# A gathering graph kernel: GpSimd starts each group of four gathers only after the group before has landed

## The reference

```
deg_out = segment_sum(edge_weight, src); deg_in = segment_sum(edge_weight, dst)
norm = edge_weight * rsqrt(deg_out[src] * deg_in[dst] + EPS)
# a layer, done twice (W6, then W7):
xt  = x @ W
msg = xt[src] * norm[:, None]
agg = segment_sum(msg, dst, num_segments=n_nodes)
h   = relu(agg + b)
```

## Time and profile before

| | us |
|---|---|
| median of three runs | 3715.28 (3714.16 to 3717.88) |
| the profiled execution, whole | 3720.0 |
| its span in the trace | 3718.2 |
| POOL busy in the span | 2172.4 (58%) |
| PE busy in the span | 3030.2 (81%) |
| granted TensorE clock, mean | 0.90 of full |

### The profile page before, as it was taken

One profiled execution on the slowest core, in us unless ns is written; L12 is line 12 of the kernel. 1 busy time (PEld: TensorE's weight loads), 2 busy tenths in 40 slices (PEclk: granted clock), 3 DMA queues, 4 the chain that ended last, 5 costly groups with the idle time before them and its releaser, 6 DMA issues.

```text
span 3718.2 us, 52328 instructions
## 1 busy us (share of the span) xinstructions
PE 3030.2 (81%) x16152; PEld 2012.8 (54%) x16152; DVE 1803.2 (48%) x4528; ACT 1150.8 (31%) x4063; POOL 2172.4 (58%) x2090
## 2 busy tenths in 40 slices
PE   4777837888888888888885689888888888888998
PEld 3445514555555555555553356556555555555666
DVE  9989835666666666656542133223212324132334
ACT  5787834444444443444330011001000101002211
POOL 4666656666666666666664666666666666630000
PEclk8899967999898998999987789989998998988999
DMA  4331134544544545445456534654655454533221
GB/s 118 99 104 54 56 77 132 159 154 138 172 139 152 161 136 170 139 140 171 129 180 186 131 123 135 204 175 145 197 189 188 152 190 151 191 104 105 78 77 47
DMA packets 219543, 515.58 MB, mean 139 GB/s; under 512 B 62465, under 2 KB 129831, under 8 KB 208169
## 3 DMA queue, kind: packets, MB, share of 16 engines
q0 software_dynamic: 88704, 243.35, 22.8%
q1 hardware_dynamic: 124053, 262.34, 20.8%
q10 hardware_dynamic: 6500, 6.40, 0.6%
HBM read 384.88 MB, written 127.07 MB: 138 GB/s over the span
## 4 chain that ended last, share of the span: by engine, by line
PE 46%; issue 8%; another core or an unknown queue 6%; DVE 3%; DMA 2%; ACT 1%; POOL 1%; DVEq 1%; ACTq 0%; SPq 0%; POOLq 0%
PE ps L702 19%; PE ps L680 7%; PE ps L663 5%; PE ps L873 5%; PE ps L886 4%; PE ps L821 1%; PE ps L824 1%; POOL ringb L1960 1%; PE ps L642 1%; PE ps L809 1%; ACT ab L1737 1%; DMA t<-mbuf 0%; DVE ab L1303 0%; DMA x2d<-accb 0%
## 5 line engine op out<-in xcount | busy, mean ns | idle before, releaser
L1960 POOL DMA_INDIRECT ringb<-t,src x1848 | 1862.5, 1008 | 979.1 <-issue 496.5
L702 PE MATMUL ps<-xb,ab 125*128 125x256 f32 (+1 forms) x4700 | 1253.7, 407 | 83.3 <-issue 80.6
L702 PEld LDWEIGHTS ps<-xb,ab 125*128 125x128 f32 x4700 | 934.9, 203 | 358.5 <-issue 197.7
L680 PE MATMUL ps<-mlb 128*125 128x300 f32 x1260 | 484.1, 475 | 170.4 <-issue 67.9
L1737 ACT ACTIVATE ab<-ps 125x250 f32 x724 | 295.2, 408 | 797.3 <-PE ps L680 408.8
L663 PE MATMUL ps<-ringb,Sb 128*32 128x257 f32 (+1 forms) x3696 | 378.2, 417 | 141.9 <-issue 78.2
L680 PEld LDWEIGHTS ps<-mlb 128*125 128x125 f32 x1260 | 228.1, 205 | 335.7 <-issue 298.1
L1933 POOL TENSOR_TENSOR ab<-ab,wn 128x100 f32<-128x100 f32 x201 | 274.6, 1371 | 167.7 <-DVE ab L1086 167.7
L604 PE MATMUL ps<-ab 128*50 128x125 f32 x3228 | 222.7, 286 | 132.3 <-ACT ab L1659 45.0
L1270 DVE TENSOR_TENSOR mlb<-iof,rel 128x900 f32<-128x900 f32 (+1 forms) x231 | 232.2, 1005 | 172.5 <-remote 104.6
L1659 ACT ACTIVATE ab<-ab,wn 128x50 f32<-128x50 f32 x1212 | 288.8, 330 | 18.6 <-DVE ab L1086 18.6
(11 more groups left out here) (245 smaller groups left out, 2704.3 us busy)
## 6 DMA issues: line engine op xcount, KB each, us to landing
ad<-ab SPq DMA_DIRECT2D x42, 1600.0 KB
ab<-ad SPq DMA_DIRECT2D x42, 1600.0 KB
ringb<-t,src POOLq DMA_INDIRECT x1848
kvd<-mlb SPq DMA_DIRECT2D x50, 256.0 KB, 2.1
kvb<-kvd SPq DMA_DIRECT2D x50, 256.0 KB
x2t<-mlb SPq DMA_DIRECT2D x13, 500.0 KB
xb<-x2t SPq DMA_DIRECT2D x13, 500.0 KB, 8.2
xb<-in_x SPq DMA_DIRECT2D x10, 625.0 KB
```

What stands on the lines that cost most here:

```text
L680: e.matmul(PS[bank_of(t)][0:R, 0:HR], low[:, slot_of(t), :], high[:, slot_of(t), :], start=True, stop=True).then_inc(s_bld, 1)
L702: ins = e.matmul(PS[dense_bank(L, d)][:, 0:wd], lhs, X[0:R, k, 0:wd], start=k == 0, stop=k == NT - 1)
L1960: e.indirect_dma_start(msg[:, slot * QT + k, 0:width], None, table, bass.IndirectOffsetOnAxis(src[:, t:t + 1], 0)).then_inc(s_g[slot], 16)
```

## The change

One condition is added in front of each quad but the first of each pass: GpSimd waits until all four gathers of the preceding quad have landed, 64 counts of the preceding slot's semaphore. The count is exact for the quad: it takes in the 41 quads that each slot held in pass 0.

```diff
--- before.py
+++ after.py
@@ -1955,6 +1955,9 @@
                         e.wait_ge(s_mm, NQ)
                     elif j == 4:
                         e.wait_ge(s_flag, 1)
+                    if j >= 1:
+                        landed = (j - 1) % RQ
+                        e.wait_ge(s_g[landed], 64 * (L * len(range(landed, NQ, RQ)) + (j - 1) // RQ + 1))
                     for k in range(QT):
                         t = column(L, j) + k
                         e.indirect_dma_start(msg[:, slot * QT + k, 0:width], None, table,
```

## The result

| | before | after |
|---|---|---|
| median | 3716.58 us (3714.16 to 3720.15) | 4827.75 us (4820.07 to 4844.52) |
| ratio | | 1.2997, 95% interval 1.2974 to 1.3019 |
| profiled execution, whole | 3720.0 us | 4833.86 us |
| its span | 3718.2 us | 4832.1 us |

The change costs 1111 us. The forecast was +765 and its range ended at 4670: the direction and the mechanism were right, the size was not.

A forecast was written before the change was run, and what follows sets the result against it. PE was taken to set the pace, GpSimd following closely. Quiet cycles 1752 + 1484 plus load 313 gave 3549 us against 2779, +770 on 3720.0: 4490, rounded to 4480 us; range 4270 to 4670 us.

The forecast's parts named there:

- between and behind the passes: Stretches before, between and after the two passes: claimed to stay as they were, their work not being touched.
- What bounds it, and the direction: Both passes: PE sets the pace, GpSimd follows closely; added waits make GpSimd's line longer, so slower by over 0.2%, 96%.
- The quiet landing: At each quad's start without SP's load: the last gather lands 1.86 us after its descriptors are written.
- The load: Landings beside SP's large transfers: 92 quads caught, each 3.4 us later, 313 us in all.
- The descriptors: GpSimd's descriptor writing with gaps: thins a little in a longer pass, to 5.02 and 4.77 us a quad.
- GpSimd's own start after a wait: From the landing to the next quad's first gather: taken as 0.24 us, bounded by 0 and 0.98 us.
- the forecast's own spread: Whole kernel: load 130 to 450 us and start 0.1 to 0.4 us, about 4250 to 4660 us, chance 78%.
- (a): Rival at the quads' starts: the wait is mostly hidden, time within 0.2% of 3715 us; chance 2%.
- (b): Rival: fewer gathers in flight let PE's large products get `A` sooner, faster at 3632 us; chance 2%.
- (c): Rival: little load on the landing, 313 us shrinking to some 60, start in 0.1 us, 4170 us; chance 10%.
- (d): Rival: a store holds the whole quad, 7 us a caught quad, start 0.4 us, 4730 us; chance 8%.
- The sign that I named wrongly: In the profile after, almost none of the waits on GpSimd's gather line would be released by PE.

The follow-up runs named there:

- e1: Changed kernel with the wait for PE's slot moved to the last gather of the quad before, so no gather has two waits: 4542.64 us.
- e2: Changed kernel with the two waits in the other order, landing written before slot: 4545.17 us.
- e5: The changed kernel timed again, unaltered, on a chip where the kernel before takes 3684.11 us: 4818.39 us.
- e9: The changed kernel timed again, unaltered, on a chip where the kernel before takes 3366.01 us: 4836.35 us.
- e10: The kernel of e1 run again, on the chip of e9 beside the changed kernel: 4540.32 us.
- e11: Changed kernel with SP's stores and loads of A cut to a sixteenth, which leaves work out: 4659.45 us against 4836.35.
- e8: Changed kernel with GpSimd also held to four quads ahead of PE in place of six: 4814.72 us beside 4818.39.
- e7: Changed kernel with the landing wait at every second quad only: 4169.68 us, +486 beside the kernel before at 3684.11.
- e3: Kernel before with a second, always satisfied wait at each quad from the seventh on: 3365.61 us beside 3366.35, ratio 0.9997.
- e4: Changed kernel with the landing wait moved from a quad's first gather to its second: 3960.19 us, 594 us over the kernel before.
- e6: Changed kernel, but each quad waits for the landing of the quad before the last one: 3727.01 us beside 3684.11, ratio 1.0123.

## Why the prediction was wrong in size

By its own steps, in the profiled executions. The measured parts of a gap are means over all quads, worked out from the trace's landing events (the last landing of a quad less the end of its fourth gather, and the next start less that landing).

| term | forecast | measured |
|---|---|---|
| descriptors and their gaps, pass 0 and 1, a quad | 5.02, 4.77 us | 5.18, 4.76 us: +37 us |
| landing in the quiet | 1.86 us | 1.8 to 1.9 us |
| landing under load, in all | 313 us | about 360 us: +48 |
| from the landing to the next gather | 0.24 us | 0.86, 0.87 us: +286 |
| between and behind the passes | 0 | -22 |

The terms add up to 349 us. The profiled execution grew by 1114 us where the sum said 770, so 344 were missing; the forecast also counted 462 waits where there are 460, which is most of the difference.

- **What bounds it, and the direction: right.** A quad's serial line is longer than the step of 6.09 and 5.93 us, GpSimd has no cover for it, and PE becomes the one that waits, 653 us at line 663 alone. "Slower", forecast with 96%, came true, and the stretches outside the passes stayed but for 22 us.
- **The quiet landing: right.** 1.86 us from the earlier trace rows came back, with a median of 1.82 to 1.88 us in each pass of the result, e1, e2, e5, e9 and e10.
- **The load: nearly right.** 313 against some 360 us. 97 of the 460 landings are more than 1 us late, by 3.4 us in the mean, where the forecast had 92 with 3.4. The 200 GB/s and the single price of 3.4 us were rough, and e11 shows that only half of it comes from the largest transfers, so part of the agreement is luck.
- **The descriptors: a small error.** They were to thin out in a longer pass. In pass 0 the mean gather went from 1.043 us to 1.067, with DVE busy 877 of 2117 us. DVE's share alone, which the forecast took as the reason, doesn't explain this.
- **The failed step is GpSimd's own start after a wait.** The prediction bounded it by 0 and 0.98 us and took 0.24, "a little under the 0.30 us between two gathers, as the added wait also is an instruction of its own". The form was seen, and its price was taken from gathers without one. 0.24 is nearly right where the gather carries the landing wait (e1, e2, the first quads): 0.26 us as a rule, 0.92 at every ninth quad, 0.33 in the mean. With the wait in an instruction of its own it is 0.76 us, and 1.71 at every ninth quad, 0.86 in the mean. 0.62 us x 460 = 286 us of the 344 us that were missing. The separate instruction is 0.53 us of this, 245 us in all; the other 42 us stay in e1 and e2. e10 takes the instruction away and gets back 296 us on the chip of e9 (e1 and e2, on another chip than the result, 285 and 283), of which some 50 are descriptors: their mean in pass 0 also falls, from 5.18 to 4.96 us a quad. Why it falls is open.
- **The range failed for the same reason.** The known bound of 0.98 us was cut to 0.4 for the forecast's own spread. 0.98 on 460 quads is 340 us more than 0.24, which alone would have taken the forecast of 4480 to 4820. The spread that was stated was also added up too low: load 450 and start 0.4 together give 4480 + 137 + 74 = 4691, not 4660. A bound far from the value taken has to stay in the range when the term is multiplied by every quad.
- **The rivals.** (a) and (b) needed a landing within 1 us and fell with it. (c), little load, fell: landings under load cost 360 us. (d) came closest in time, 4730 us, but not by its mechanism: a late landing is late by 3.4 us in the mean, and by 7.2 at the most. PE's pace as a part of it is excluded by e5 and e9, and by e8 for the ring.
- **The sign that I named wrongly.** I expected almost no wait released by PE. The profile shows 136; by e1 they are landings with the wrong name.

What stays open: why every ninth start takes longer. It takes 0.95 us more in the changed kernel (and in e7, at the 25 of these quads that wait) and 0.66 us more in e1, e2 and e10, so it belongs to a start behind a landing and not to the separate instruction alone. e3, where nothing is waited for, has no such start. Nothing in these runs names its cause.

No version that does all the work is faster than the kernel before.

## What to carry to other kernels

Price a wait in a tight issue loop as the whole exposed line, the landing, plus the start after it, times every round, and see what lies beside the landing: one more gather in flight (e4) took away 60% of the loss and one more quad (e6) nearly all, on a chip where GpSimd had slack. Where an instruction gets a second wait, put the one that is expected to end last onto the instruction itself (here the one written first), or give the other to an earlier instruction; here the order of two lines was worth 6% of the time. A kernel whose pace differs by chip should be forecast from the line that the change makes serial, not from the distance to the time before: 4830 us held on every chip, a ratio of 1.30 to 1.44 did not.

## What the runs showed of the hardware

- A wait in an instruction of its own costs GpSimd 0.5 us more than the same wait carried by the gather if it is the last to be satisfied (0.76 against 0.26 us from the landing to the start; 1.71 against 0.92 at every ninth quad), and nothing if it is satisfied while descriptors are being written (e3: 0.9997).
- A gather of 128 rows of 1 KB lands 1.8 to 1.9 us after its descriptors are written in the quiet, with one quad allowed in flight (median 1.84 us in the changed kernel) as with six (1.80 in the kernel before); beside SP's stores and loads of `A` it is up to 9 us (the longest wait of the changed kernel is 10.0 us with its start).
- The same kernel before takes 3366, 3684 and 3716 us on different chips, with a mean granted clock of 0.92 to 0.93 on the fastest and 0.90 in the trace of the slowest. The kernel that waits for its gathers, timed beside 3366, 3684 and 3716 us, does not share in this: 4818 to 4836 us, although its granted clock is only 0.82 to 0.83.
